# Attention with all sixteen heads' products for the maxima in one group, and one maximum operation over them

## The reference

```python
q = (layernorm(x) @ Wq.T + bq) * 16 ** -0.5      # heads of 16 features
k, v = ctx @ Wk.T + bk, ctx @ Wv.T + bv
scores = jnp.einsum('bhqd,bhkd->bhqk', q, k)     # 128 x 128 for each batch and head
attn = jax.nn.softmax(scores, axis=-1)
x = x + jnp.einsum('bhqk,bhkd->bhqd', attn, v) @ Wo.T + bo
# then: logits = layernorm(x) @ router_w.T + router_b; the expert with the largest logit;
# y = relu(relu(h @ w1[e] + b1[e]) @ w2[e] + b2[e]); x = x + y
```

## Time and profile before

| | us |
|---|---|
| median of three runs | 1454.6 |
| the profiled execution, its own time | 1464.87 |
| span of its trace, first to last instruction | 1463.1 |
| PE busy | 1250.0 (85%) |
| DVE busy | 1020.0 (70%) |
| ACT busy | 783.1 (54%) |
| POOL busy | 667.6 (46%) |

### The profile page before, as it was taken

The page is one execution under the profiler, slowest core; times in us unless marked ns, Lnnn a source line. Parts: engine busy times, 40 slices in busy tenths (PEclk is TensorE's granted clock), DMA queues, the critical chain, the costliest instruction groups (busy, mean ns, idle before and its releaser), DMA issues. The chain is left out here.

```text
span 1463.1 us, 43093 instructions
## 1 busy us (share of the span) xinstructions
PE 1250.0 (85%) x15172; PEld 892.3 (61%) x15173; DVE 1020.0 (70%) x2867; ACT 783.1 (54%) x1602; POOL 667.6 (46%) x811
## 2 busy tenths in 40 slices
PE   4999999899989998999899899999973388777776
PEld 3666666666656665666666666666652266656654
DVE  3678888878878887888688878888876244433342
ACT  3566666656656665666466656666644133333332
POOL 4344444434444553454344434454424155545554
PEclk9999999989999999999999999999986599999998
DMA  2611221111111111212121111111100655566542
GB/s 96 220 45 60 65 98 61 61 60 60 60 61 60 60 67 53 67 67 86 36 93 68 60 60 60 60 60 60 45 17 34 168 172 173 181 175 178 153 134 67
DMA packets 87297, 126.60 MB, mean 87 GB/s; under 512 B 11521, under 2 KB 69132, under 8 KB 87054
## 3 DMA queue, kind: packets, MB, share of 16 engines
q1 hardware_dynamic: 67678, 68.97, 16.5%
q0 software_dynamic: 19440, 55.15, 10.2%
HBM read 68.95 MB, written 59.31 MB: 88 GB/s over the span
## 5 line engine op out<-in xcount | busy, mean ns | idle before, releaser
L587 DVE TENSOR_REDUCE mx<-scores 128x8 bf16<-128x1024 f32 x256 | 307.7, 1222 | 40.6 <-PE scores L814 38.4
L466 ACT ACTIVATE pv<-scores 128x1024 f32<-128x1024 f32 x256 | 248.2, 1021 | 79.9 <-PE scores L836 79.9
L392 POOL DMA_INDIRECT out<-work x160 | 157.9, 987 | 163.6 <-DVE work L752 115.3
L458 ACT ACTIVATE mxT<-b 128x128 bf16<-128x128 f32 x128 | 35.5, 277 | 306.4 <-PE b L821 306.4
L360 POOL DMA_INDIRECT pages<-row,slot_i x128 | 129.0, 1008 | 80.1 <-issue 53.6
L855 PE MATMUL b<-wo_s,work 128*128 128x256 f32 x512 | 148.4, 413 | 19.1 <-DVE work L604 19.1
L846 PE MATMUL b<-pv 128*32 128x128 f32 x4096 | 143.3, 279 | 14.0 <-issue 10.5
L829 PE MATMUL scores<-qM,kT 32*128 32x256 f32 x2048 | 152.2, 410 | 0.1
L1008 PE MATMUL scores<-pv,zt 128*128 x320 | 116.9, 450 | 35.0 <-issue 14.7
L752 DVE SCALAR_TENSOR_TENSOR work<-scores,work 128x256 f32<-128x256 f32 x160 | 67.6, 422 | 101.6 <-PE scores L1008 61.1
L544 ACT ACTIVATE row<-b 128x256 f32<-128x256 f32 x160 | 61.0, 381 | 141.4 <-PE b L991 97.0
(11 more groups left out here) (121 smaller groups left out, 2556.3 us busy)
## 6 DMA issues: line engine op xcount, KB each, us to landing
work<-pages SPq DMA_DIRECT2D x40, 520.0 KB
xs<-x_in SPq DMA_DIRECT2D x32, 512.0 KB, 5.9
work<-ctxT SPq DMA_DIRECT2D x32, 512.0 KB, 7.2
pages<-empty POOLq DMA_DIRECT2D x30, 520.0 KB, 6.3
row<-w SPq DMA_DIRECT2D x160, 64.5 KB
pages<-empty POOLq DMA_DIRECT2D x1, 5200.0 KB, 23.2
out<-work POOLq DMA_INDIRECT x160
pv<-w SPq DMA_DIRECT2D x1, 2080.0 KB
```

Source lines behind the costliest of these rows:

```text
L392: pool.indirect_dma_start(out_rows, bass.IndirectOffsetOnAxis(pr[:, r, COL_TOKEN:COL_TOKEN + 1].bitcast(U32), 0), pr[:, r, 0:D], None, bou ...
L466: act.activation(pt[:, u % 2, 2 * p:2 * p + 2], scores4[:, 1024 * p:1024 * (p + 1)].rearrange("p (j k) -> p j k", j=2), ACT.Exp).then_inc( ...
L587: dve.tensor_reduce(mx[:, u % 2, 8 * p:8 * (p + 1)], scores4[:, 1024 * p:1024 * (p + 1)].rearrange("p (h k) -> p h k", h=8), AX.X, ALU.max ...
```

## The change

`scores_for_max` and `maxima` lose their parameter `p`: all sixteen matmuls of a batch are issued as one group, and one DVE operation reduces all four banks (128 x 2048 elements to 128 x 16). Both stand at the beginning of the batch's own slot. The semaphores `S_done` and `max_out` count four in a step, not eight.

```diff
-            def maxima(q, u, p, at):
-                if p == 0 and (at >= 1 or u >= 2):
+            def maxima(q, u, at):
+                if at >= 1 or u >= 2:
                     qq, uu = (q, u - 2) if u >= 2 else (q - 1, u + 2)
                     after(dve, "mxT_done", 4, qq, uu)
-                after(dve, "S_done", 8, q, 2 * u + p)
-                dve.tensor_reduce(mx[:, u % 2, 8 * p:8 * (p + 1)], scores4[:, 1024 * p:1024 * (p + 1)].rearrange("p (h k) -> p h k", h=8),
+                after(dve, "S_done", 4, q, u)
+                dve.tensor_reduce(mx[:, u % 2, 0:16], scores4[:, :].rearrange("p (h k) -> p h k", h=16),
                                   AX.X, ALU.max).then_inc(S["max_out"], 1)
...
                     if has(at, 0):
-                        maxima(s, u, 1, at)
+                        maxima(s, u, at)
...
                         residual(q1, k1 % 2, k1, u1, at1)
-                    if u < 3 and has(at, 0):
-                        maxima(s, u + 1, 0, at)
-                    elif u == 3 and has(at, 1):
-                        maxima(s + 1, 0, 0, at + 1)
...
-            def scores_for_max(q, par, u, p):
+            def scores_for_max(q, par, u):
                 for c in range(2):
                     for m in range(2):
-                        for j in (2 * p, 2 * p + 1):
+                        for j in range(4):
...
                         after(pe, "exp_out", 8, q1, 2 * u1 + 1)
                     if has(at, 0):
-                        scores_for_max(s, par, u, 1)
+                        scores_for_max(s, par, u)
...
-                    if u < 3 and has(at, 0):
-                        after(pe, "exp_out", 8, s, 2 * u)
-                        scores_for_max(s, par, u + 1, 0)
-                    elif u == 3 and has(at, 1):
-                        after(pe, "exp_out", 8, s, 2 * u)
-                        scores_for_max(s + 1, 1 - par, 0, 0)
```

More of the change, by code:

```diff
@@ L710, in _ @@
             dve.tensor_tensor(bo_s[:, :], b7[:, 0:D], bo_s[:, :], ALU.add).then_inc(S["bo_ready"], 1)
-            maxima(0, 0, 0, 0)
             def step(s, k, at):
@@ L818, in max_transpose @@
             def max_transpose(q, u):
-                after(pe, "max_out", 8, q, 2 * u + 1)
+                after(pe, "max_out", 4, q, u)
                 for j in range(4):
@@ L901, in _ @@
             ins.then_inc(S["bvo_done"], 1)
-            scores_for_max(0, 0, 0, 0)
             def step(s, k, at):
```

## The result

The changed kernel takes 1462.6 us, the median of six runs (1461.1 to 1467.6), and the kernel before, run beside it, 1454.9 (1450.2 to 1459.7). The medians differ by 7.7 us; the ratio worked out from all the runs is 1.006, with an interval of 1.0034 to 1.0087, which is 8.7 us (5 to 13). The forecast had said slower, by 17.4 us, to 1472: the right way, and twice the size.

A forecast was written before the change was run, and what follows sets the result against it. PE bounds slots 3 and 1, DVE slot 2; after the change DVE's chain decides. 28 x 0.73 = 20.4 us, -5.0 at loop returns, +2.5 in steps 0 to 2: 17.9, scaled to 1472 us, range 1458 to 1497.

The forecast's parts named there:

- DVE becomes the later one: Every slot: DVE's chain lets `project_out` start 4.68 us behind the products for the maxima, PE arrives at 4.2; about 0.5 later.
- The sixteen in about 0.40 us: Head of each slot on PE: sixteen matmuls on four row groups take about 0.40 us, so nothing is added for them.
- What PE saves behind `project_out`: PE after `project_out`: dropping eight matmuls saves 0.34 us per slot, 0.12 more in slots 3 and 1; 1.6 a step.
- What DVE's chain adds: Start of products to `project_out`: the whole 2.25 us maximum now precedes `attend_copy`; net 0.73 us more in each step.
- Steps 0 to 2: First steps, some PE work missing: DVE's longer chain shows fully; about 2.5 us lost, with the small excess of the rest.
- Returns of the loop: Five slots 0 after a loop return: DVE catches up, its 0.67 overrun doesn't count, the 0.34 saved does; -5.0 us.
- Slot 2: DVE's stall runs until 0.96 us behind POOL's L324, which is tied to L684 of slot 1; length 9.88 us, was 9.95.
- L678 and slot 1: Slot 1 on DVE: L678 ends with POOL's L334 at 4.89 us, residual starts at 7.73; length 7.64 us, was 7.57.
- The gain through slot 2: Slot 2: the 1.06 us stall goes if tied to the maxima's second half; 32 us saved, 1440 us; chance 0.10.
- The doubled sixteen: Slots 3 and 1: the sixteen matmuls take twice as long, 0.34 us more each; 19 us, 1491 us; chance 0.10.
- the cheaper maximum: DVE's pieces shrink by 0.2 us in each slot, so the sum is even: 1455 us; chance 0.05.
- more contention: POOL's long operations meet more of DVE's, or the clock falls: another 1 us a step lost, 1500 us; chance 0.07.

## Why the prediction was right, and where not

- *PE nearly full, DVE not far behind; DVE becomes the later one.* Shown. L849 waits for L604 in every slot, in slots 3 and 1 4.72 us behind S where 4.68 was forecast; the wide maximum takes 2.29 us (start to start 2.21, I took 2.25), and starts 0.53 us behind S, not 0.44, with sixteen products ahead of its signal, not eight. Together that is the 0.04 between the two. With half of the keys the three slots shrink as the chain says.
- *The sixteen in about 0.40 us.* 0.41. But four row groups are not the reason, as the order by pairs shows.
- *What PE saves behind `project_out`.* This is the term that was mis-sized. Forecast 0.46, 0.34, 0.46 and 0.34 us (slots 3, 0, 1, 2), measured 0.65, 0.34, 0.64 and 0.49: 2.12 us in a step instead of 1.60. The group of eight put back costs 0.54 in slots 1 and 3, not 0.46, and 0.50 in slot 2, not 0.34; the rest lies in the work beside it (in slot 1 0.97 us from L849 to the projection, where the earlier trace rows gave 1.06 to the next work, and 1.81 from the projection to S, where it had been 1.90: 546.89 less 544.65 less the 0.34 of the group).
- *What DVE's chain adds.* Forecast 2.33 us in a step (its 0.73 and the 1.60 saved), measured 2.63 (the L855 to L849 differences of the table). With the point above, a step grew by 2.63 - 2.12 = 0.51 us, and not by 0.73: 28 x 0.22 = 6 us of the miss.
- *Steps 0 to 2.* Forecast 2.5 us lost. Measured, step 0 has gained 2.8 us by its slot 1, and in the last slot of step 3 the changed kernel is still 2.1 us ahead. That is 4.6 us more of the miss; which part of the first step gave it wasn't tried.
- *Returns of the loop.* Forecast -5.0. The pauses of PE there add up to 7.1 us. From the last slot of step 3 to that of step 31 the changed kernel loses 5.2 us: 28 x 0.51 = 14.3 less 9.1 at the returns and at the end, against 20.4 - 5.0 forecast. Across the five returns the two traces' difference moves by -3.3, -0.5, 0.0, -1.8 and -0.9 us, so uneven that a part may be the chance of two single executions.
- *Slot 2.* The length was right (9.85, forecast 9.88) for a wrong reason, so in part by luck. I tied the stall to L324, and it now ends at 549.05 us, over a microsecond ahead of L324. The plain transfers show that it belongs to L360. L324 starts as the fourth L360 ends, so its start marked the same moment, and what I had tied it to (L684 of slot 1) is what starts the scatters. The forecast's length survived because the stall moved from behind the maxima to ahead of them and kept its size of 1.04 us.
- *L678 and slot 1.* Right to the hundredth: it was to end with L334, 4.89 us behind S, and the residual to start at 7.73. L334 ends at 543.96, L678 at 544.00, or 4.89 behind 539.11, and L612 starts at 546.84, or 7.73. The row is only shorter (0.30 us instead of 1.11), since DVE came to it later. With half of the keys DVE comes earlier, and it lasts 1.38 us to the same end.
- *The rivals.* The gain through slot 2 did not come, since the stall does not belong to the place of the second half of the maxima. The doubled sixteen is ruled out by its 0.41 us, the cheaper maximum by 2.21 us where it needed 2.05, and more contention by the same granted clock of 0.98 and the shorter L678; in the runs that shorten slots 0 and 1 contention does come back, through L334. By the Trainium skill's page VectorE: DVE Perf Modes, section on the TRN2 errata, one operation saves 0.125 us, an estimate; the runs with one and with two differ by 0.07 in a slot. The rule of the Trainium skill's page TensorEngine Tiling (Array Packing), section PSUM Bottleneck, held in slots 3, 0 and 1: PE's busy time fell, and DVE's reading of the products from PSUM, with the chain behind it, decided.

The attention ends 3.2 us later in the traces, and the timed runs say 8.7 us with an interval of 5 to 13. In the traces the miss is 17.9 - 3.2 = 14.7 us, of which the step gives 6, steps 0 to 2 give 4.6, and the returns with the end 4.1. The few us between 3.2 and 8.7 may lie in the spread of single executions; that stays open.

## What to carry to other kernels

Fewer and wider operations can lose when they put the whole of a reduction between an engine and what waits for it: ask what the first half was doing while the engine was busy elsewhere, and add up the chain from the start of the group to the next consumer before you count saved overhead. Where the chain wins, put work that is ready into the wait and move what makes the other engine late; both together turned this change from 0.6% slower into 0.9% faster. A slot that answers to no edit of its engines is held by something else: take the suspect away before pricing gains that pass through it, and ask which engine's chain starts the suspect: what slots 0 and 1 won here was waited for in slot 2.

## What the runs showed of the hardware

- Four indirect transfers issued in a row by POOL (0.97 to 1.12 us each) go with stalls of DVE that wait for PE's finished work. With plain transfers in their place the stall is gone. In the changed kernel it ends 0.80 to 0.93 us behind the start of the third in 21 of 27 steps (549.05 after 548.14), and 1.5 in the other six. Where it stands ahead of `attend_copy`, as in the kernel before, it ends 1.9 to 2.0 us behind the start of the fourth (551.23 after 549.29; L324 starts as the fourth ends); with half of the keys there is one of each. In the set with the kernel before at 1364.7 us it was absent with the same scatters, on a chip that had shown it. PE pauses too, mostly by 0.3 to 0.5 us at a time, without a wait that the profile shows. Whether that or late signals make DVE's stall of 1.0 us, and why not always, stays open.
- A small DVE operation can last until a long POOL operation ends: 2.61 us for 128x4 elements beside L324, 1.11 us for 128x32 beside L334. That it can cost a step 3.4 us I had not expected. The Trainium skill states it in SBUF — State Buffer, section SBUF: two separate sides: DVE in a two-port mode and POOL share a pair of ports, which the one that starts first keeps for its whole instruction. The trace agrees for L678, which starts 1.28 us behind L334 and ends 0.03 behind it. With the cast of 2.61 us the order is less plain: its row starts 0.23 us ahead of L324's and ends 0.03 behind it. That these operations run in a two-port mode no run here shows.
- A group of eight matmuls of 32x128 between others of 128 rows costs 0.54 us in slots 1 and 3, 0.50 in slot 2 and 0.34 in slot 0, a wait for the exponentials included, though its rows show 0.40; sixteen in one group last 0.41.
